# The second layer norm moved tile by tile from the seam between two layers into the attention loop

## The reference

```python
# x: (8, 4096, 1024); 16 heads; layer norm without scale or shift, eps 1e-5
x = x + layernorm(attention(layernorm(x)))     # Wq, Wk, Wv, Wo, bo
x = x + layernorm(ffn(layernorm(x)))
# attention: here the softmax runs over the 8-row sequence axis after a transpose per position
# ffn: a gated recurrence over the leading axis, 8 steps:
#   f = sigmoid(xt@wf.T + c@uf.T + bf); i = sigmoid(xt@wi.T + c@ui.T + bi)
#   g = tanh(xt@wc.T + c@uc.T + bc);    c = f*c + i*g
# then h = tanh(x@wo.T + c_final@uo.T + bo)
```

## Time and profile before

| | us |
|---|---|
| runs shown (two), the metric | 3496.4 and 3651.48, median 3573.94 |
| the profiled execution, the metric | 3500.74 |
| its span on the slowest core (core 4) | 3499.2 |
| spans of the eight cores | 3475.0 to 3499.2 |
| share of the span in which TensorE, VectorE, ScalarE, GpSimd are busy | 55%, 29%, 16%, 10% |

### The profile page before, as it was taken

The page is one execution under the profiler, slowest core; times in us unless marked ns, Lnnn a source line. Parts: engine busy times, 40 slices in busy tenths (PEclk is TensorE's granted clock), DMA queues, the critical chain, the costliest instruction groups (busy, mean ns, idle before and its releaser), DMA issues.

```text
span 3499.2 us, 31721 instructions; the slowest of 8 cores (3475.0 to 3499.2 us)
## 1 busy us (share of the span) xinstructions
PE 1931.8 (55%) x9395; PEld 925.5 (26%) x9540; DVE 1014.3 (29%) x1754; ACT 554.3 (16%) x1257; POOL 333.7 (10%) x510
## 2 busy tenths in 40 slices
PE   1666455555454554544543012999999996886000
PEld 0323222232232222322321011444444442332000
DVE  0434233343343333433422023211221221222222
ACT  1011111111111111111111065211111111111000
POOL 1010101001101011011021100000000001111111
PEclk9766566666666666666656555999999998998555
DMA  7010211111212111112121865000000003111333
GB/s 118 23 48 23 57 44 47 35 43 49 52 40 58 43 47 48 38 43 56 33 62 60 129 170 165 1 11 3 12 13 13 13 13 63 31 31 51 120 120 114
DMA packets 167406, 186.99 MB, mean 53 GB/s; under 512 B 109886, under 2 KB 122174, under 8 KB 167230
## 3 DMA queue, kind: packets, MB, share of 16 engines
q0 software_dynamic: 53456, 151.38, 16.8%
q1 hardware_dynamic: 113792, 33.57, 4.0%
HBM read 151.68 MB, written 58.72 MB: 60 GB/s over the span
## 4 chain that ended last, share of the span: by engine, by line
PE 51%; DVE 15%; DMA 11%; issue 9%; ACT 7%; another core or an unknown queue 4%; DVEq 1%; POOL 1%; ACTq 0%; POOLq 0%; SPq 0%
PE ps_p L1581 11%; PE ps_a L2038 10%; PE ps_a L2044 10%; DMA xin<-x 7%; PE ps_p L1445 5%; PE ps_p L2131 3%; PE ps_p L2138 3%; DVE otn L1747 3%; PE ps_a L1698 2%; DMA vst<-v_scr 2%; DVE qst L1650 2%; DVE kst L1650 2%; PE ps_rl L1731 2%; ACT pt_sb L1710 2%
## 5 line engine op out<-in xcount | busy, mean ns | idle before, releaser
L1710 ACT ACTIVATE pt_sb<-ps_a 128x512 bf16<-128x512 f32 x128 | 76.0, 594 | 1022.4 <-PE ps_a L1698 1022.4
L1731 PE MATMUL ps_ot<-pt_sb,vst 128*65 128x128 bf16 x256 | 63.1, 278 | 294.2 <-DMA vst<-v_scr 247.9
L2058 ACT ACTIVATE gat<-ps_a,biases 128x512 f32<-128x512 f32 x192 | 132.0, 687 | 584.4 <-PE ps_a L2044 584.4
L2068 DVE TENSOR_TENSOR cT<-cT,gat 128x512 f32<-128x512 f32 x64 | 44.3, 693 | 579.8 <-ACT gat L2058 579.8
L1581 PE MATMUL ps_p<-wq_sb,xlnT_t 128*128 128x512 bf16 x481 | 170.0, 526 | 44.3 <-DVE xlnT_t L1567 43.0
L1445 PE MATMUL ps_p<-wo_sb,zlT_t 128*128 128x512 bf16 x482 | 159.8, 503 | 59.7 <-DVE zlT_t L1431 59.2
L2038 PE MATMUL ps_a<-xtT_sl,wq_sb 128*128 128x512 bf16 x500 | 132.6, 409 | 50.7 <-DMA xtT_sl<-xt_scr 38.9
L2131 PE MATMUL ps_p<-qst,gat 128*128 128x512 bf16 x495 | 120.1, 383 | 59.6 <-DMA gat<-xt_scr 33.9
L1682 POOL DMA_DIRECT2D vst<-v_scr x128 | 96.0, 755 | 533.8 <-DMA v_scr<-vtok 468.9
L2044 PE MATMUL ps_a<-zb,wk_sb 128*128 128x512 bf16 x500 | 125.3, 392 | 0.8 <-issue 0.2
L2138 PE MATMUL ps_p<-kst,zb 128*128 128x512 bf16 x508 | 121.8, 382 | 0.3
(11 more groups left out here) (159 smaller groups left out, 2738.3 us busy)
## 6 DMA issues: line engine op xcount, KB each, us to landing
xin<-x POOLq DMA_DIRECT2D x96, 512.0 KB, 4.8
xin<-xr POOLq DMA_DIRECT2D x32, 512.0 KB, 4.1
x<-x1t POOLq DMA_DIRECT2D x32, 512.0 KB, 3.0
out<-x1t POOLq DMA_DIRECT2D x32, 512.0 KB, 3.2
v_scr<-vtok SPq DMA_DIRECT2D x32, 256.0 KB, 2.1
vst<-v_scr POOLq DMA_DIRECT2D x128, 64.0 KB, 3.2
od<-orow SPq DMA_DIRECT2D x128, 64.0 KB, 1.8
zin<-od POOLq DMA_DIRECT2D x128, 64.0 KB, 3.2
```

Of the source, the lines that this page charges most:

```text
L1710: ch_exp.inc(sc.activation(pt_sb[:, gbuf * 512:(gbuf + 1) * 512], ps_a[:, abank * 512:(abank + 1) * 512], AF.Exp, scale=0.125))
L1731: inst = t.matmul(psot[0:65, pk4 * 128:(pk4 + 1) * 128], vst[:, vslot * 260 + pk4 * 65: vslot * 260 + (pk4 + 1) * 65], pt_sb[:, gbuf * 512 ...
L2058: ch_gev.inc(sc.activation(gat[:, gi * 512:(gi + 1) * 512], ps_a[:, pg * 512:(pg + 1) * 512], func, bias=biases[:, bcol + mt:bcol + mt + 1]))
```

## The change

LN3 becomes a function `emit_LN3(tt)`, defined ahead of the attention loop. Inside the loop it is called at groups 2, 6, 10 and 14 of batches 2 to 7, for the tiles of the batch two before (24 tiles). In the tail it is called for tiles 24, 25 and 26 between the last four `emit_P2` calls, and for tiles 27 to 31 after them. The barrier on all engines is removed, and the wait for the weights with it: only `f_cinit` still waits for `FCONSTS`. The load of a tile waits for the x1 stores of its own batch (`sto_hist`), and the normalisation into `xln_sb` for the last reader of that buffer (`xln_hist`), which may be a store to `xt_scr`. The statistics of LN3 write both by-products to `sqj` and so have one more drain (`dr=True`). The weight issues `g_fc1` to `g_fc3` keep their place behind the attention part in the file, so on GpSimd they come after the x1 load of tile 31.

```diff
 def ln_stats_sc(P, ch_rst, xi, sq_junk, sq_junk2, sl, s1, s2, mean, msq,
-                rstd, width, wait=None):
+                rstd, width, wait=None, dr=False):
...
         sc.activation(sq_junk, xi, AF.Square, accum_out=s2[:, sl])
+        if dr:
+            sc.drain()
         sc.activation(sq_junk2, xi, AF.Copy, accum_out=s1[:, sl])
...
         if rt == 3:
             p2_zld_hist[n] = (ch_zld[0].n, ch_zld[1].n)
+            sto_hist[n] = ((ch_sto[0], ch_sto[0].n), (ch_sto[1], ch_sto[1].n))
...
+    def emit_LN3(tt):
+        buf = tt % 2
...
+        def f_l3(s, tt=tt, xi=xi, chx=chx, need=xin_last[buf],
+                 stw=sto_hist[tt // 4]):
+            if need:
+                s.wait_ge(ch_vfree.sem, need)
+            s.wait_ge(stw[0][0].sem, stw[0][1])
+            s.wait_ge(stw[1][0].sem, stw[1][1])
+            chx.inc(s.dma_start(out=xi, in_=x1[tt * 128:(tt + 1) * 128, :]))
+        P("gpsimd", f_l3)
...
+        ln_stats_sc(P, ch_rst, xi, sqj[:], sqj[:], sl, s1, s2, mean,
+                    msq, rstd, D, wait=(chx, chx.n), dr=True)
+
+        def f_ap3(v, xi=xi, xl=xl, sl=sl, rs=ch_rst.n, xh=xln_hist[buf]):
+            v.wait_ge(ch_rst.sem, rs)
+            if xh:
+                for c_, n_ in xh:
+                    v.wait_ge(c_.sem, n_)
+            ch_xln.inc(v.tensor_scalar(xl, xi, mean[:, sl], rstd[:, sl],
+                                       AL.subtract, AL.mult))
+            ch_vfree.inc(v.drain())
+        P("vector", f_ap3)
...
+        def f_t3(t, xl=xl, trb=trb, xc=ch_xln.n, tev=ch_trevx[trb].n):
+            t.wait_ge(ch_xln.sem, xc)
+            t.wait_ge(ch_trevx[trb].sem, tev)
+            for ft in range(8):
+                inst = t.transpose(ps_trx[trb][:, ft * 128:(ft + 1) * 128],
+                                   xl[:, ft * 128:(ft + 1) * 128], ident_sb[:])
+            ch_trx[trb].inc(inst)
+        P("tensor", f_t3)
...
+        def f_te3(v, buf=buf, trb=trb, trc=ch_trx[trb].n):
...
+        P("vector", f_te3)
...
+        def f_s3(s, tt=tt, buf=buf, cht=ch_trd[buf], tev=TRE):
...
+        P("sync", f_s3)
...
+            if grp % 4 == 2 and n >= 2:
+                emit_LN3(4 * (n - 2) + grp // 4)
             if grp % 4 == 3 and n >= 1:
                 emit_P2(n - 1, grp // 4, ODS_hist[n - 1])
...
-    for rt in range(4):
-        emit_P2(B - 1, rt, ODS_hist[B - 1])
+    emit_P2(B - 1, 0, ODS_hist[B - 1])
+    emit_LN3(24)
+    emit_P2(B - 1, 1, ODS_hist[B - 1])
+    emit_LN3(25)
+    emit_P2(B - 1, 2, ODS_hist[B - 1])
+    emit_LN3(26)
+    emit_P2(B - 1, 3, ODS_hist[B - 1])
+    for tt in range(27, 32):
+        emit_LN3(tt)
...
-    for _eng in ("tensor", "scalar", "vector", "sync"):
-        def f_barrier(e, bar=_bar):
...
-    P("gpsimd", f_barrier_g)
...
+    def f_fmemset(v):
+        v.drain()
+        v.memset(onesf[:], 1.0)
+        v.memset(onesr2[:], 1.0)
+    P("vector", f_fmemset)
```

More of the change, by code:

```diff
@@ L83, in ln_stats_sc, with f_stat @@
 def ln_stats_sc(P, ch_rst, xi, sq_junk, sq_junk2, sl, s1, s2, mean, msq,
-                rstd, width, wait=None):
-    def f_stat(sc, xi=xi, sl=sl, wait=wait, sq_junk2=sq_junk2):
+                rstd, width, wait=None, dr=False):
+    def f_stat(sc, xi=xi, sl=sl, wait=wait, sq_junk2=sq_junk2, dr=dr):
         if wait is not None:
@@ L1376, in build_fused_program @@
     NPK = 64
-    tr_hist = []
     exp_hist = []
@@ L1513, in build_fused_program @@
     ODS_hist = {}
+    sto_hist = {}
+    xln_hist = {0: None, 1: None}
+    ch_trd = (c("trd0", 16), c("trd1", 16))
+    def emit_LN3(tt):
+        buf = tt % 2
+        xi = xin[:, buf * D:(buf + 1) * D]
+        xl = xln_sb[:, buf * D:(buf + 1) * D]
+        sl = slice(buf, buf + 1)
+        chx = ch_xd[buf]
+        def f_l3(s, tt=tt, xi=xi, chx=chx, need=xin_last[buf],
[6 more added lines that the diff above has]
+        P("gpsimd", f_l3)
+        chx.bump()
+        ln_stats_sc(P, ch_rst, xi, sqj[:], sqj[:], sl, s1, s2, mean,
[9 more added lines that the diff above has]
+        P("vector", f_ap3)
+        ch_xln.bump()
+        ch_vfree.bump()
+        xin_last[buf] = ch_vfree.n
+        trb = tr_slot()
+        def f_t3(t, xl=xl, trb=trb, xc=ch_xln.n, tev=ch_trevx[trb].n):
[6 more added lines that the diff above has]
+        P("tensor", f_t3)
+        ch_trx[trb].bump()
+        def f_te3(v, buf=buf, trb=trb, trc=ch_trx[trb].n):
+            v.wait_ge(ch_trx[trb].sem, trc)
+            ch_trevx[trb].inc(v.tensor_copy(xln_sb[:, buf * D:(buf + 1) * D],
+                                            ps_trx[trb][:]))
+        P("vector", f_te3)
+        ch_trevx[trb].bump()
+        TRE = (ch_trevx[trb], ch_trevx[trb].n)
+        def f_s3(s, tt=tt, buf=buf, cht=ch_trd[buf], tev=TRE):
+            s.wait_ge(tev[0].sem, tev[1])
+            cht.inc(s.dma_start(
+                out=xt_scr[:, tt * 128:(tt + 1) * 128].rearrange(
+                    "(ft p) r -> p ft r", p=128),
+                in_=xln_sb[:, buf * D:(buf + 1) * D].rearrange(
+                    "p (ft r) -> p ft r", ft=8)))
+        P("sync", f_s3)
+        ch_trd[buf].bump()
+        xln_hist[buf] = ((ch_trd[buf], ch_trd[buf].n),)
@@ L1536, in f_apply @@
         def f_apply(v, xi=xi, xl=xl, sl=sl, rs=ch_rst.n,
-                    trneed=(tr_hist[gti - 2] if gti >= 2 else None)):
+                    xh=xln_hist[buf]):
             v.wait_ge(ch_rst.sem, rs)
-            if trneed:
-                v.wait_ge(trneed[0].sem, trneed[1])
+            if xh:
+                for c_, n_ in xh:
+                    v.wait_ge(c_.sem, n_)
             ch_xln.inc(v.tensor_scalar(xl, xi, mean[:, sl], rstd[:, sl],
@@ L1562, in emit_P1_front @@
         ch_trx[trb].bump()
-        tr_hist.append((ch_trx[trb], ch_trx[trb].n))
+        xln_hist[buf] = ((ch_trx[trb], ch_trx[trb].n),)
         def f_trev(v, xt=xt, trb=trb, trc=ch_trx[trb].n):
@@ L1829, in build_fused_program @@
     A_STO = (ch_sto[0].n, ch_sto[1].n)
-    _bar = tuple((_bc, _bc.n) for _bc in _chans if _bc.n > 0)
-    for _eng in ("tensor", "scalar", "vector", "sync"):
-        def f_barrier(e, bar=_bar):
-            for _c2, _n2 in bar:
-                e.wait_ge(_c2.sem, _n2)
-        P(_eng, f_barrier)
     w_sb = {"wf": wq_sb, "uf": wk_sb, "wi": wv_sb, "ui": wo_sb,
@@ L1903, in build_fused_program @@
     FCONSTS = ch_cd.n
-    def f_barrier_g(g, bar=_bar):
-        for _c2, _n2 in bar:
-            g.wait_ge(_c2.sem, _n2)
-    P("gpsimd", f_barrier_g)
     NT2 = S // 128
[L1911 to L1986, removed]
@@ L2194, in build_fused_program, with f_xl2 @@
         ot = x1t[:, buf * D:(buf + 1) * D]
-        def f_xl2(s, rt=rt, xi=xi, chx2=ch_xd[buf], need=(ch_ho.n - 1)):
+        def f_xl2(s, rt=rt, xi=xi, chx2=ch_xd[buf], need=(ch_ho.n - 1),
+                  xl_=(xin_last[buf] if rt < 2 else 0)):
             if rt >= 2 and need > 0:
                 s.wait_ge(ch_ho.sem, need)
+            if xl_:
+                s.wait_ge(ch_vfree.sem, xl_)
             chx2.inc(s.dma_start(out=xi, in_=x1[rt * 128:(rt + 1) * 128, :]))
```

1 line of the change is left out of this document (removed).

## The result

The changed kernel takes 3479.16 us (median), the kernel before 3500.74 us measured beside it; the ratio is 0.9919 with a 95% interval of 0.9893 to 0.9946, so 0.8% faster, and no change by the 2% bound. Forecast were 3477 us and a range of 3452 to 3512.

What follows compares the result with a forecast made beforehand. Bound taken as a 242.7 us seam of weights, then LN3, with chained attention work. Seam gives back 124.6 us, attention takes 86, tail 15: net -23.6 from 3500.74, so 3477 us, range 3452 to 3512.

Steps and rivals of the forecast that it cites:

- The seam: Stretch from last x1 store to recurrence: 242.7 us, weights 84.8 then LN3 149.7; the change gives back 124.6.
- A tile in the attention: LN3 tile between two attention groups: moves the next by 3.6 us, 24 tiles +86 us, bounds 77 to 110.
- the twin: emit_P1_front at groups 5 and 11, existing layer norm with the same first steps, used to price a tile.
- No wait for the x1 load in the attention: LN3's x1 load in the attention lands near 1120 us, 5 us before its statistics could start.
- `xin` for the residual in time: Residual load in the following emit_P2 waits for LN3's normalisation in the same buffer, at no cost.
- the rival of the late load: Attention: x1 loads land late and ScalarE waits with the next exponential; slower, 3537 us at 3 us late; chance 0.05.
- The extra drain: Drain added to LN3's statistics in the attention: about 0.2 us of slack, so no cost.
- Absorption: Rival: the attention's idle time hides the tiles, 1.3 us each, 31 us in all, time 3422 us; chance 0.06.
- The tail: Tiles 24 to 26 between the last emit_P2 calls: 5.0 us each, +15 us, bounds 9 to 21.
- Weights held back: Five x1 loads ahead of the weights on GpSimd: weights start 19.2 us after the last store, +18.6 us.
- Transfers beside the weights: Last tiles' stores and first two xtT_sl loads run beside the weights: sum 10, taken as +8 us (0 to 12).
- After the weights: Weights' count, cast and start of TensorE before the recurrence: 6.1 us, replacing 6.4.

Runs made afterwards that it cites:

- all_tail: Changed kernel with all 32 LN3 tiles behind the last Wo block, ahead of the weights, none in the attention; 3529.26 us in one execution.
- weights_early: Changed kernel with the second layer's weights issued early, in the Wo blocks of the last batch and the tail; 3407.49 us, ratio 0.9742 to the kernel before.
- split: Changed kernel with each attention LN3 tile's transposes, copy back and store moved one group later; 3432.14 us, ratio 0.9806 to the kernel before.
- hosted: Changed kernel with LN3 tiles placed whole inside Wo blocks, five tiles behind, tiles 27 to 31 staying behind; ratio 0.9678 to the kernel before.
- tail_plain: Changed kernel with tiles 24, 25 and 26 behind the last Wo block instead of between the blocks; 3482.78 us in a single execution.
- xt_wait: Changed kernel with the first two xtT_sl loads waiting until the weights have landed; 3474.32 us, ratio 0.9896 to the kernel before.
- full: Changed kernel with LN3 tiles inside the next Wo block, one behind, only tile 31 left, and weights early; 3308.47 us, ratio 0.9444 to the kernel before.

## Why the prediction was right, and where it was not

- **The seam is weights and LN3 one after the other.** Right: `all_tail` keeps both exposed and stays at 251.8 us; the changed kernel hides 27 tiles, `weights_early` the weights as well, and each gains.
- **A tile in the attention costs TensorE's wait for the normalisation.** The mechanism was right, and the twin was the right row: 3.69 - 0.23 = 3.46 us at the site (forecast 3.6). `split` removes the wait and with it more than half the price. The term was 10 us too large, 75.7 instead of 86, mostly because I stopped at the start of the next scores. The chain runs to the next exponential, and the scores behind the eight transposes took 0.63 us instead of 0.96. That pays back 0.33 in each tile. Why they are shorter is not shown.
- **No wait for the x1 load in the attention; `xin` for the residual in time.** Right, by the 0.50 us between exponential and statistics; the rival of the late load is out. The extra drain costs nothing there.
- **Absorption.** This rival did not come: a tile cost 3.15 us and not 1.3. The idle time it counts on is real all the same: `hosted` finds it behind the Wo blocks. The place decides, not the share of idle time.
- **The tail.** 18.7 us instead of 15, inside the bounds. The row of 3.6 us from load to statistics was too kind: beside the four `zin` loads it was 5.4 (1952.97 to 1958.38), and the transposes of `zin` came 11.73 us after the store instead of 5.53. `tail_plain` gives it all back.
- **Weights held back.** 21.0 instead of 19.2, for the same reason: from the load of tile 27 to its statistics it was 4.8 us (2033.74 to 2038.58) instead of 3.6.
- **Transfers beside the weights.** 10.4 us for the last matrix; my 8 was a choice below the 10 the rows gave. `xt_wait` shows that 8.3 of it are the `xtT_sl` loads, for which I had put 6. `all_tail` has the same cost with nothing hidden.
- **After the weights.** 6.2 (2149.62 to 2155.80) instead of 6.1.
- **The sum.** -25.6 on core 4 against -23.6. The terms missed by -10, +4, +2 and +3, and mostly cancel; that the sum came so close is in part luck. The core that is read matters as well: over the eight cores the recurrence starts 13.6 to 46.4 us earlier, 28.9 in the mean. The measured ratio, 0.8% or 28 us, fits that mean; but of the 48 us by which core 4 got shorter in the two profiled executions, 22 lie behind the recurrence, where the change does nothing (below).

## What to carry to other kernels

When a piece of work is moved into a loop whose engines run their lists in order, its price is the wait that it puts between two neighbours, read off the nearest row that already has this shape. Idle shares say only that a free place exists. Look for the place where every engine that the piece needs already stands still for another reason: here the same 27 tiles cost 94 us in one place and nothing in the other. Then move the issue of large transfers to where their buffers come free, and not to where the file happens to reach them; and look first for the small stores beside them that an engine waits for, since in `full` VectorE stood 23 us for such stores.

## What I had not expected of the hardware

The last stage, a loop of one load, one store and two VectorE operations for each of 32 tiles, runs at a speed that goes by pairs of neighbouring cores and changes from execution to execution. In all nine profiled executions the two cores of a pair took the same time for it within 5 us, while pairs of one execution lay up to 29 us apart (539 and 568 us in `all_tail`). Stretch 3280 to 3440 us, by engine, granted clock, DMA share, GB/s: first core 4 of the kernel before, then core 4 and core 0 of the changed one.

```profile
3280.00:3440.00 160.00, 0.00 (x0) 0.00 (x0) 38.12 (x38) 0.00 (x0) 19.12 (x36) 0.50 0.35 118
```

```profile
3280.00:3440.00 160.00, 0.00 (x0) 0.00 (x0) 40.75 (x40) 0.00 (x0) 21.23 (x40) 0.50 0.37 131
```

```profile
3280.00:3440.00 160.00, 0.00 (x0) 0.00 (x0) 36.66 (x36) 0.00 (x0) 19.02 (x36) 0.50 0.36 121
```

In 160 us VectorE has 38, 40 and 36 operations. From the start of the output product to the last store the cores 0 to 7 of the changed kernel took 554, 555, 537, 536, 538, 537, 538 and 537 us, those of the kernel before 560, 558, 538, 542, 559, 555, 553 and 548, and in `full` cores 4 and 5 took 561 and 560 and all others about 540. So some 20 us of the metric are decided there by which pair is slow, as much as this change is worth. What makes a pair slow was not tried.
